# Transposed attention scores contracted over the 32 rows of their own head pair

## What is computed

```
q = layernorm(x) @ Wq.T + bq ; k, v = ctx @ Wk.T + bk, ctx @ Wv.T + bv      # heads of 16
attn = softmax(einsum('bhqd,bhkd->bhqk', q, k) / 4)
x = x + tanh(g_xattn) * (einsum('bhqk,bhkd->bhqd', attn, v) @ Wo.T + bo)
h = bit_linear(layernorm(x), w1)           # round(x*127/max|x|) times ternary weights, 1024 wide
h = silu(depthwise_conv1d(h, 3 taps) + conv_b)
x = x + tanh(g_ffn) * bit_linear(h, w2)
```

## Time and profile before

| | us |
|---|---|
| median of 3 runs | 258.36 |
| the runs | 256.16, 258.36, 260.51 |
| span of the profiled execution | 258.7 |
| TensorE matmuls busy | 206.8 (80%) |
| TensorE weight loads busy | 121.7 (47%) |
| VectorE busy | 191.1 (74%) |
| ScalarE busy | 143.2 (55%) |
| GpSimd busy | 81.0 (31%) |
| mean granted TensorE clock | 0.894 |

### The profile page before, as it was taken

The page is one execution under the profiler, slowest core; times in us unless marked ns, Lnnn a source line. Parts: engine busy times, 40 slices in busy tenths (PEclk is TensorE's granted clock), DMA queues, the critical chain, the costliest instruction groups (busy, mean ns, idle before and its releaser), DMA issues. The chain is left out here.

```text
span 258.7 us, 3024 instructions
## 1 busy us (share of the span) xinstructions
PE 206.8 (80%) x972; PEld 121.7 (47%) x972; DVE 191.1 (74%) x344; ACT 143.2 (55%) x205; POOL 81.0 (31%) x74
## 2 busy tenths in 40 slices
PE   8497899988899968998998789989967089521675
PEld 3264357563665636285465453763645057100243
DVE  1626866878348987869699677786955877999864
ACT  1111224112558679847586598476889416895241
POOL 0120432003325760306156503152670320365000
PEclk9979999999979989799999597999977779965789
DMA  7990000000000000000200000002000000100002
GB/s 237 398 322 0 0 4 0 0 0 3 0 0 0 1 3 0 1 0 4 81 0 0 0 0 0 0 0 81 0 3 0 0 1 26 55 1 0 0 3 81
DMA packets 5372, 8.43 MB, mean 33 GB/s; under 512 B 480, under 2 KB 4704, under 8 KB 4976
## 3 DMA queue, kind: packets, MB, share of 16 engines
q1 hardware_dynamic: 4896, 6.38, 7.0%
q10 hardware_dynamic: 464, 1.90, 2.1%
HBM read 6.18 MB, written 2.10 MB: 32 GB/s over the span
## 5 line engine op out<-in xcount | busy, mean ns | idle before, releaser
L1079 POOL TENSOR_TENSOR hid<-hid,right 128x512 f32<-128x512 f32 x32 | 42.3, 1326 | 49.3 <-DVE hid L668 36.3
L668 DVE SCALAR_TENSOR_TENSOR hid<-u,par,hid 128x512 f32<-128x512 f32 x32 | 37.4, 1177 | 0.0
L363 PEld LDWEIGHTS ps_ox<-vbd,probs 128*128 128x128 f32 x256 | 31.0, 194 | 7.3 <-issue 7.1
L926 ACT ACTIVATE hid<-u,par 128x512 f32<-128x512 f32 x32 | 23.0, 718 | 17.4 <-PE ps_h L452 8.9
L363 PE MATMUL ps_ox<-vbd,probs 128*128 128x34 f32 x256 | 30.7, 276 | 1.7 <-DVE o_s L623 1.6
L1039 POOL TENSOR_TENSOR rstd<-var,minus_half 128x4 f32<-128x4 f32 (+1 forms) x6 | 9.7, 1616 | 50.6 <-DVE minus_mean L639 40.5
L953 ACT ACTIVATE hid<-hid,round_off 128x1024 f32<-128x1024 f32 x12 | 13.6, 1150 | 21.4 <-DVE hid L714 21.4
L935 ACT ACTIVATE hid<-hid,par 128x512 f32<-128x512 f32 x32 | 22.3, 709 | 3.1 <-POOL hid L1079 3.1
L430 PE MATMUL ps_h<-w1q 128*128 128x512 bf16 x48 | 16.2, 473 | 9.4 <-ACT hid L935 8.2
L930 ACT ACTIVATE right<-u,par 128x512 f32<-128x512 f32 x32 | 22.6, 707 | 0.0
L714 DVE TENSOR_TENSOR hid<-hid,ps_ox 128x1024 f32<-128x1024 f32 x16 | 18.5, 1216 | 2.5 <-PE ps_ox L401 2.2
(11 more groups left out here) (121 smaller groups left out, 353.2 us busy)
## 6 DMA issues: line engine op xcount, KB each, us to landing
x_s<-x SPq DMA_DIRECT2D x4, 512.0 KB, 13.9
out<-x_s SPq DMA_DIRECT2D x6, 256.0 KB, 2.2
w2f<-w_t ACTq DMA_DIRECT2D x1, 1024.0 KB, 10.2
w_attn<-attn_w SPq DMA_DIRECT2D x1, 1024.0 KB, 10.5
w1f<-w_t SPq DMA_DIRECT2D x1, 1024.0 KB, 12.5
cT<-ctx_t ACTq DMA_DIRECT2D x1, 512.0 KB, 4.1
out<-x_s SPq DMA_DIRECT2D x4, 128.0 KB, 1.8
row<-rows ACTq DMA_DIRECT2D x1, 256.0 KB, 5.9
```

The lines of the kernel that those rows point to most:

```text
L363: last = nc.tensor.matmul(o_ps[:, k, 2 * e:2 * e + 2, :], probs[:, g % 2, e, k * P:(k + 1) * P], vbd[:, 2 * g + e, :], start=True, stop=True)
L668: nc.vector.scalar_tensor_tensor(out=hid[:, f, :], in0=u[:, f % US, 0:N], scalar=par[:, CW + 3 * f:CW + 3 * f + 1], in1=hid[:, f, :], op0= ...
L926: nc.scalar.mul(hid[:, f, :], u[:, f % US, 1:N + 1], par[:, CW + 3 * f + 1:CW + 3 * f + 2]).then_inc(mid_ready, 1)
L1079: nc.gpsimd.tensor_tensor(hid[:, f, :], hid[:, f, :], right[:, f % RIGHTS, :], ALU.add).then_inc(conv_ready, 1)
```

## The change

`mx` gets 128 columns a tile, zeroed once, and `row_max` writes the 16 maxima so that after the transpose the maxima of a pair lie among the 32 rows on which its queries and keys lie (rows 32i to 32i+31 for pair i of a chunk; column 2c + e for chunk c, head e of the pair). `neg_max` gets 128 rows. `ind` becomes 128 x 2 x 128, ones in the row that belongs to the pair's head. Both matmuls of `scores_t` contract over these 32 rows; the two `ind` matmuls of a group come first, then the two `kbd` matmuls. Constants and counts follow; no wait is added or taken out.

```diff
+ROWS = 2 * HD
+IN_CHUNK = PAIRS // DC
...
-        indf = sb("indf", [HEADS, PAIRS * P])
-        ind = sb("ind", [HEADS, PAIRS, P], BF16)
+        indf = sb("indf", [P, DC * P])
+        ind = sb("ind", [P, DC, P], BF16)
...
-        mx = sb("mx", [P, T, HEADS])
-        neg_max = sb("neg_max", [HEADS, N], BF16)
+        mx = sb("mx", [P, T, P])
+        neg_max = sb("neg_max", [P, N], BF16)
...
+        mx_heads = mx[:].rearrange("p t (i x) -> p t i x", x=ROWS)[:, :, :, 0:2 * DC]
...
-                    last = nc.tensor.transpose(ps_o[0:HEADS, k * P:(k + 1) * P], mx[:, k, :], idf[:])
+                    last = nc.tensor.transpose(ps_o[:, k * P:(k + 1) * P], mx[:, k, :], idf[:])
...
                 for e in range(2):
-                    j = 2 * g + e
-                    c, h = j * 2 // HC, j * 2 % HC
-                    nc.tensor.matmul(slots[g % 2][:, e, :], ind[:, j, :], neg_max[:], start=True, stop=False)
-                    last = nc.tensor.matmul(slots[g % 2][:, e, :], kbd[:, c, h:h + 2, :], qT[:, c, :],
+                    c, i = (2 * g + e) // IN_CHUNK, (2 * g + e) % IN_CHUNK
+                    rows = slice(i * ROWS, (i + 1) * ROWS)
+                    nc.tensor.matmul(slots[g % 2][:, e, :], ind[rows, c, :], neg_max[rows, :], start=True, stop=False)
+                for e in range(2):
+                    c, i = (2 * g + e) // IN_CHUNK, (2 * g + e) % IN_CHUNK
+                    rows = slice(i * ROWS, (i + 1) * ROWS)
+                    last = nc.tensor.matmul(slots[g % 2][:, e, :], kbd[rows, c, 2 * i:2 * i + 2, :], qT[rows, c, :],
                                             start=False, stop=True)
...
-                nc.vector.tensor_reduce(mx[:, k, :], s_slots[k % 3][:].rearrange("p c (h k) -> p (c h) k", k=KEYS),
-                                        AX.X, ALU.max).then_inc(mx_ready, 1)
+                nc.vector.tensor_reduce(
+                    mx_heads[:, k].rearrange("p i (c e) -> p i c e", c=DC),
+                    s_slots[k % 3][:].rearrange("p c (i e k) -> p i c e k", i=IN_CHUNK, k=KEYS),
+                    AX.X, ALU.max).then_inc(mx_ready, 1)
...
+            nc.vector.memset(mx[:], 0.0).then_inc(zeroed, 1)
+            dve.wait_ge(zeroed, 10)
...
-                nc.scalar.mul(neg_max[:], ps_o[0:HEADS, :], -1.0).then_inc(neg_ready, 1)
+                nc.scalar.mul(neg_max[:], ps_o, -1.0).then_inc(neg_ready, 1)
...
-    pair_ind = np.repeat(np.eye(HEADS, dtype=np.float32), KEYS, axis=1)
+    pair_ind = np.zeros((IN_CHUNK, ROWS, DC, 2, KEYS), np.float32)
+    for c in range(DC):
+        for e in range(2):
+            pair_ind[:, 2 * c + e, c, e] = 1.0
+    pair_ind = pair_ind.reshape(P, DC * P)
```

More of the change, by code:

```diff
@@ L835, in _ @@
             nc.vector.memset(minus_half[:], -0.5).then_inc(zeroed, 1)
-            dve.wait_ge(zeroed, 9)
+            nc.vector.memset(mx[:], 0.0).then_inc(zeroed, 1)
+            dve.wait_ge(zeroed, 10)
             nc.vector.memset(vbd[0:KEYS, :, HD:VW], 1.0).then_inc(zeroed, 1)
@@ L843, in _ @@
             dve.wait_ge(ident_in, 16)
-            dve.wait_ge(zeroed, 11)
-            nc.vector.tensor_copy(ind[:].rearrange("h j k -> h (j k)"), indf[:]).then_inc(consts_ready, 1)
+            dve.wait_ge(zeroed, 12)
+            nc.vector.tensor_copy(ind[:].rearrange("p c k -> p (c k)"), indf[:]).then_inc(consts_ready, 1)
             nc.vector.tensor_copy(idh[:], idf[:]).then_inc(consts_ready, 1)
@@ L1013, in _ @@
             act.wait_ge(par_in, 16 * PAR_DMAS)
-            act.wait_ge(zeroed, 9)
+            act.wait_ge(zeroed, 10)
             nc.scalar.activation(tg[:], par[:, G:G + 2], ACT.Tanh).then_inc(tg_ready, 1)
@@ L1096, in step @@
                     residual_base(front)
-            pool.wait_ge(zeroed, 9)
+            pool.wait_ge(zeroed, 10)
             root(var[:, 0:1], rstd[:, 0:1], var1_ready, 1, rstd1_ready)
@@ L1102, in _ @@
             spread_keys(Turn(0))
-            pool.wait_ge(zeroed, 11)
+            pool.wait_ge(zeroed, 12)
             spread_values(Turn(0))
```

## The result

The changed kernel takes 264.81 us (median of 4 runs, 262.14 to 269.71) against 259.44 us of the kernel before (4 runs, 256.16 to 262.06): a ratio of 1.021, 95% interval 1.014 to 1.027. It is slower by some 2%, where I had forecast 3% faster. The profiled execution spans 263.6 us, before 258.7. Some runs of a kernel are over 1.5% longer than its fastest; all ratios here go by the other runs, and of the profiled executions used further down those of e2_fill32, e8_fill_more and e11_order_fill are such longer ones.

What follows compares the result with a forecast made beforehand. TensorE was taken as the bound from 33.8 to 51.5 us, VectorE from 75.2 to 93.3. Forecast: 258.7 - 8.7 (blocks) + 0.2 (start) + 1.0 (clock) = 251.2 us profiled, 250.8 median; range 247 to 256.

Steps and rivals of the forecast that it cites:

- the clock: TensorE's granted clock, 1.2 or 2.4 GHz, falls behind thin stretches; 1.0 us charged, ends 0 and 5.
- A score group: `scores_t`, two head pairs on TensorE: from 2.7 to 1.74 us by partial overlap, 1.0 us less over 16 groups.
- rival D: Score groups overlap fully, in two stream lengths: 1.30 us a group, 249.4 us in all; chance 0.07.
- Blocks: Stretches where transposed scores are computed; gains 3.5, 0, 0.75, 1.5, 0.75, 1.5 and 0.7, sum 8.7 us.
- second block: 59.5 to 75.2 us, two groups: gain 0, as `values(1)` waits for `o_s`; 2 us become TensorE idle time.
- third: 75.2 to 93.3 us, two groups: gain 0.75 us, VectorE's wait for `hidden(2)`; from there VectorE is the bound.
- fourth: 103 to 118 us, two groups: second exponential and `rden` start sooner, `top` at 112.25 instead of 113.74; gain 1.5 us.
- waits of 1.71 gone: Sign of a right forecast: VectorE's wait of 1.71 us for TensorE, before `rden` at 111.89, disappears.
- The added parts: Wider transposes, reordered reduction, memset taken as free or hidden; larger `pair_ind` load delays the start, 0.2 us charged.
- rival C: Shorter 32-row groups let the clock fall in the first block; 2% slower needs eight falls, 264 us; chance 0.08.
- first block: 28.4 to 51.5 us, four groups, TensorE the bound: 4.0 us less a new 0.4 wait for `xn`, gain 3.5.
- rival B: Sharing rows wins nothing: records run in turn or wait for loads, 2.40 or 2.31 us a group; 254.8 us; chance 0.25.

Runs made afterwards that it cites:

- e2_fill32: The changed kernel with filler matmuls whose result nobody reads, on rows 0 to 31, where TensorE waits: 266.44 us, ratio 1.032.
- e8_fill_more: The changed kernel with unread 128-row filler matmuls where TensorE waits, 14 of them around `hidden(4)` and `hidden(5)`: 250.99 us, ratio 0.971.
- e11_order_fill: The kernel before with both `ind` matmuls first in a group and unread 128-row fillers: runs of 249.75, 254.05, 254.44 and 254.58 us, no interval.
- e9: The kernel before with only the order in a group changed, both `ind` matmuls ahead of both `kbd` matmuls: 254.80 us, ratio 0.986.
- e3: The changed kernel's layout, but both kinds of matmul in a group contract over all 128 rows, without overlap: 252.53 us, ratio 0.979.
- e7: The changed kernel's layout with only the `ind` matmuls on 32 rows, `kbd` contracting over 128 again: 251.79 us, ratio 0.977.
- e6: The changed kernel with every pair of a group taken from rows 0 to 31, so pairs can't overlap: 278.29 us, ratio 1.080.

## Why the prediction was wrong

The sum failed at its last term, the clock: 1.0 us was charged, and the clock took more than all that the groups gave. The other terms, in the order of the prediction:

- **A score group.** Right in the mechanism, that pairs on different rows overlap, and mis-sized: forecast 1.74 us, measured 1.21 for one alone (from 130.27, the next matmul at 131.48) and 1.26 to 1.50 for two in a row. What was wrong here is the order of issue. I had let the other pair's first record wait until the first pair's second one starts. In the rows above two records start at 28.94, one of each pair, and the two others at 29.37, one stream later: what stands on other rows passes what waits for its own. In the loop group 1's `ind` matmuls (106.32) start 0.2 us ahead of the `kbd` matmuls of group 0 (106.52), behind which they stand in the program, so four pairs run at once. That is rival D's 1.30 us a group, to which I gave 0.07, and more. It is an error in the kernel's favour, and does not explain the loss.
- **Changes of shape.** 0.27 us a pair in the forecast; e9, which saves two changes a group, saves 2.7 - 2.45 = 0.25 us, about as assumed there.
- **Blocks.** At the places where ScalarE or VectorE was said to set the pace, they do. In the second block `values(1)` starts 9.9 us behind the first group in both traces (59.52 to 69.43, 62.40 to 72.30), and TensorE's wait before it rose from 1.14 to 2.61 us, forecast about 3: no gain, as said. In the third, `scores` wait only 1.05 us for `qT`, where they waited 2.24 in the kernel before; the block is 2.1 us shorter, which only makes up for the 2.1 lost ahead of it. In the fourth, forecast to gain 1.5 us, `values(0)` starts 1.8 us sooner after the first group and takes 1.76 longer (3.63 for 1.87), so `rden` still waits 1.68 us: the sign "waits of 1.71 gone" failed through the clock.
- **The added parts.** 1.22 us for the reduction, as before; the wider transposes take 0.60 us for four, as before (a load of theirs takes 140 ns, before 90, and is hidden). The 0.2 us for `pair_ind` can't be told: `project_k` starts at 13.01 instead of 12.82, but over all runs at 12.47 to 13.33 with the larger `pair_ind` and at 12.74 to 13.42 without. e3, which has all of the added parts, is at 0.979.
- **The clock.** This is the step that failed, and by far. I charged 1.0 us, with 5 as the end, and dismissed rival C with the sentence that the 16-row matmuls of now stand at full clock. They do, but between `kbd` matmuls of 128 rows, which the change cut too. e7, with only `ind` on 32 rows, has a clock of 1.00 in the first block; with `kbd` on 32 rows as well it is 0.59 (e6, no overlap) and 0.63 (the changed kernel). In the first block alone: it lasted 22.27 us from the first group to the first scores of the next batch, was forecast at 18.8, and takes 53.57 - 28.71 = 24.86, some 6 us more, with 17 us at the lower clock. That the clock falls behind stretches in which TensorE does little could be seen in the trace of before. That streams on 32 rows are such a stretch even when they follow each other without a gap could not, and I took a busy TensorE to be safe; only the runs show it.
- **Rival C's number.** It names 264 us for eight falls, and 264.81 were measured. The mechanism is C's, but the number is in part luck: eight was what a loss of 2% needs, not a count of what would come, and D's larger gain stands on the other side.
- **Sign.** If the 8.7 us forecast as gained were all there at full clock, the clock took 8.7 - 0.2 + 4.9 = 13.4 us, with the span's 4.9 us more; the groups' larger gain would make it more. This is a remainder and not a measurement. The nearest run to it is e8, with the same groups and the clock held in more places: 250.99 us, where the forecast was 250.8. That they are so close bears the size of the gain out, but not its terms one by one.

The Trainium skill, "TensorE: Matmul & The Clock Gate", Part 3, "What overlaps and what doesn't", says that matmuls start and end strictly in program order. The starts at 106.32 and 106.52 differ from that, and there the measurement decides. The same place, read strictly, lets a weight load overlap only with matmuls on other rows, which was half of my rival B; no run here bears that out: the second records of e3, on the same 128 rows, start every 0.44 us, and those on the same 32 rows 0.43 us behind the first (28.94 and 29.37).

## What to carry to other kernels

Before matmuls of a kernel are cut to fewer rows, look at whether they are what holds TensorE's clock: with its score groups on 32 rows, a TensorE that was busy 21.8 of 23.1 us ran at 1.2 GHz for 17 of them, and fillers on 32 rows were worth nothing (1.032 with them, 1.021 without). Put the ones that share a shape next to each other first (0.986 for one exchanged loop), and take the overlap only where matmuls of all 128 rows surround it or can be filled in. A saving on TensorE that ends in a wait for another engine wins nothing and can cost: behind the wait of 3.94 us the clock was down and `values(0)` took 3.63 us, and with 128-row fillers in that wait 1.97.

## What the runs showed of the hardware

- The granted clock: fillers of the same count and columns brought much of it back with 128 rows (0.850, ratio 0.991) and not with 64 (0.812, 1.034) or 32 (0.806, 1.032); 48 clock-keeping matmuls of 512 columns cut from 128 to 32 rows cost 6.2%. The same streams one behind the other, on 32 rows and on 128, had 0.59 and 1.00 in the first block. Whether four overlapping streams on all 128 rows hold it was not settled.
- Four head pairs on four sets of 32 rows, in four banks, in bf16 and then fp32, ran at once: 1.26 us for work that takes 4.3 on 128 rows (2 x 2.15). Matmuls on other rows start ahead of ones that stand before them in the program and wait for their own rows (106.32 and 106.52).
- The cost of going between 16 and 128 rows and back is about 0.27 us a pair, and two `ind` matmuls of 0.22 us on different sets of rows overlap though the matmuls behind them take all 128 (0.32 us to the first of these, on the same rows 0.53).
